# Row-normalised graph product: the adjacency matrix in two slots of 8 MB instead of four of 4 MB, the last wide chunk in half pieces

## The reference

```
N, D, P_DROP = 8192, 64, 0.1
keep = (u >= P_DROP).astype(x.dtype)         # x, u: (8192, 64); adj: (8192, 8192), all float32
x_drop = x * keep / (1.0 - P_DROP)
y = x + jnp.matmul(adj, x_drop)
m = jnp.mean(y, axis=-1, keepdims=True)
v = jnp.var(y, axis=-1, keepdims=True)
return (y - m) / jnp.sqrt(v + 1e-05)
```

## Time and profile before

| | before |
|---|---|
| median of 3 runs | 648.95 us (648.95 to 649.85) |
| profiled execution | 649.06 us |
| its span, first to last instruction | 647.3 us |
| TensorE busy | 503.3 us (78%) |
| VectorE, ScalarE busy | 54.1 us, 17.5 us |
| read from HBM, mean rate | 272.63 MB, 424 GB/s |
| mean granted TensorE clock | 0.953 |

### The profile page before, as it was taken

How to read it: one execution, slowest core, us unless ns; L and a number is a source line. 1 busy time by engine, 2 the same in 40 slices (tenths; PEclk the granted TensorE clock), 3 DMA queues, 4 the chain that set the end, 5 groups by cost and what they waited for, 6 DMA issues and landing times.

```text
span 647.3 us, 5204 instructions
## 1 busy us (share of the span) xinstructions
PE 503.3 (78%) x2308; PEld 177.6 (27%) x2308; DVE 54.1 (8%) x104; ACT 17.5 (3%) x39; POOL 1.3 (0%) x11
## 2 busy tenths in 40 slices
PE   0588878877887977977878877887878868788796
PEld 0132322222222222322222222222322313232463
DVE  1930100001010010100001010010100101000010
ACT  0001000000000000000000000000000000000000
POOL 0000000000000000000000000000000000000000
PEclk9988998899889898899899899889988999889999
DMA  9999999999999999999999999999999999999995
GB/s 369 439 422 437 433 424 435 434 425 432 435 427 433 435 427 431 437 427 431 435 429 436 431 429 429 437 429 429 437 429 429 435 432 427 439 429 425 427 418 233
DMA packets 11817, 274.86 MB, mean 425 GB/s; under 512 B 1312, under 2 KB 1440, under 8 KB 3104
## 3 DMA queue, kind: packets, MB, share of 16 engines
q1 hardware_dynamic: 11088, 272.63, 98.2%
q10 hardware_dynamic: 720, 2.10, 0.8%
HBM read 272.63 MB, written 2.10 MB: 424 GB/s over the span
## 4 chain that ended last, share of the span: by engine, by line
DMA 78%; PE 20%; SPq 1%; issue 0%; another core or an unknown queue 0%; DVE 0%; ACT 0%; DVEq 0%; ACTq 0%
DMA piece<-adj 74%; PE acc L149 20%; DMA piece<-adj_last 4%; SPq L112 0%; SPq L124 0%; PE lifted L208 0%; SPq L109 0%; SPq L108 0%; ACT std L265 0%; DVE rows L335 0%; ACT sums_T L258 0%; DVE stats L329 0%; PE lifted L211 0%; DVE moments L331 0%
## 5 line engine op out<-in xcount | busy, mean ns | idle before, releaser
L149 PE MATMUL acc<-piece,xdrop 128*64 128x512 f32 (+1 forms) x2176 | 486.4, 602 | 139.8 <-DMA piece<-adj 137.4
L149 PEld LDWEIGHTS acc<-piece,xdrop 128*64 128x64 f32 x2176 | 161.6, 143 | 452.7 <-issue 298.7
L303 DVE SCALAR_TENSOR_TENSOR y<-folded,x_sb 128x256 f32<-128x256 f32 (+1 forms) x16 | 6.7, 417 | 555.1 <-PE folded L161 555.1
L229 ACT COPY sums_T<-acc 128x512 f32<-128x512 f32 x15 | 8.8, 585 | 372.0 <-PE acc L149 372.0
L161 PEld LDWEIGHTS folded<-fold,sums_T 128*128 128x128 f32 x124 | 15.0, 191 | 12.1 <-issue 12.1
L161 PE MATMUL folded<-fold,sums_T 128*128 128x64 f32 x124 | 17.2, 281 | 0.0
L221 ACT ACTIVATE std<-square_sum,eps 128x4 f32<-128x4 f32 (+1 forms) x16 | 4.8, 297 | 172.2 <-DVE square_sum L310 172.2
L314 DVE TENSOR_TENSOR rows<-y,rstd 128x256 f32 (+2 forms) x16 | 6.7, 417 | 1.6
L307 DVE TENSOR_TENSOR squares<-y 128x256 f32<-128x256 f32 (+1 forms) x16 | 6.7, 416 | 0.6
L310 DVE TENSOR_REDUCE square_sum<-squares 128x4 f32<-128x256 f32 (+1 forms) x16 | 6.6, 412 | 0.5
L289 DVE SCALAR_TENSOR_TENSOR xdrop<-xdrop,x_sb 128x1024 f32<-128x1024 f32 x4 | 4.9, 1220 | 13.5 <-DMA xdrop<-u 13.5
(11 more groups left out here) (23 smaller groups left out, 5.2 us busy)
## 6 DMA issues: line engine op xcount, KB each, us to landing
piece<-adj SPq DMA_DIRECT2D x60, 4096.0 KB, 31.5
piece<-adj_last SPq DMA_DIRECT2D x1, 3328.0 KB, 28.1
piece<-adj_last SPq DMA_DIRECT2D x1, 2176.0 KB, 31.3
x_sb<-x SPq DMA_DIRECT2D x1, 2048.0 KB, 7.8
xdrop<-u SPq DMA_DIRECT2D x1, 2048.0 KB, 12.2
piece<-adj_last SPq DMA_DIRECT2D x1, 1920.0 KB, 26.5
piece<-adj_last SPq DMA_DIRECT2D x1, 1792.0 KB, 26.4
out<-rows ACTq DMA_DIRECT2D x3, 512.0 KB, 14.8
```

The costliest lines, as they stand in the source:

```text
L149: last = nc.tensor.matmul(acc[i][D * h:D * h + D, 0:cols], xdrop[:, k, :], piece[:, b, :], start=(k < 2), stop=(k >= NB - 2))
L229: nc.scalar.copy(sums_T[:, i, :], acc[i][:, :]).then_inc(sums_copied, 1)
L303: nc.vector.scalar_tensor_tensor(out=y[:, 0:nj, :], in0=folded[i][:, 0:nj, :], scalar=1.0 / KEEP, in1=x_sb[:, bass.ds(block0, nj), :], op0 ...
```

## The change

Each chunk comes in two pieces of 32 blocks instead of four of 16: loads of 8192 KB, 128 rows of 64 KB, in two slots of 64 KB of every partition. The memory taken is the same. A load waits for the piece that lay in its slot one chunk earlier, as before, so one later load can stand in the queue while TensorE works, instead of three. Chunk 14, the last wide one, comes in four half pieces of 4096 KB with a semaphore each (`half_in`); both halves of a slot wait for the whole piece that lay there, and TensorE reports each half done. So the parts of chunk 15 are released after every 16 blocks, as before. The parts keep their sizes and their order; since two slots' parts now lie in one, a row of `adj_last` is 64 KB apart from the next, and was 32 KB. The centring at the start keeps its four quarters. Loads in all: 28 of 8192 KB, 4 of 4096 KB and 15 parts, where there were 60 of 4096 KB and 15 parts.

```
@@ -10,7 +10,7 @@
-SLOTS = 4
+SLOTS = 2
 PB = NB // SLOTS
 NARROW = 2
 LAST_J = J // NARROW
@@ -23,8 +23,12 @@
-PARTS = ((26, 6), (15, 17), (14, 11, 7), (2, 8, 6, 5, 4, 3, 2, 2))
+QUARTERS = 4
+QB = NB // QUARTERS
+HALVES = QUARTERS // SLOTS
+
+
+PARTS = ((26, 6, 15, 17), (14, 11, 7, 2, 8, 6, 5, 4, 3, 2, 2))
...
@@ -113,14 +118,22 @@
             for s in range(SLOTS):
                 load(0, s)
-            with sp.Fori(1, CHUNKS - 1) as c:
+            with sp.Fori(1, CHUNKS - 2) as c:
                 for s in range(SLOTS):
 
                     sp.wait_ge(piece_used, c * SLOTS + (s + 1 - SLOTS))
                     load(c, s)
+
+            for q in range(QUARTERS):
+                s, h = q // HALVES, q % HALVES
+                if h == 0:
+                    sp.wait_ge(piece_used, (CHUNKS - 3) * SLOTS + s + 1)
+                sp.dma_start(pieces[s][:, h * QB:h * QB + QB, :],
+                             adj[(CHUNKS - 2) * SLOTS + s, :, h * QB:h * QB + QB, :]).then_inc(half_in[q], 16)
             for n, (s, b, size) in enumerate(parts):
-                if b == 0:
-                    sp.wait_ge(piece_used, (CHUNKS - 2) * SLOTS + s + 1)
+
+                if b % (LAST_PB // HALVES) == 0:
+                    sp.wait_ge(piece_used, (CHUNKS - 2) * SLOTS + s * HALVES + b // (LAST_PB // HALVES) + 1)
                 sp.dma_start(narrow[s][:, b:b + size, :], adj_last[s, :, b:b + size, :]).then_inc(part_in[n], 16)
...
@@ -169,7 +182,7 @@
             for s in range(SLOTS):
-                pe.wait_ge(dropped, s + 1)
+                pe.wait_ge(dropped, (s + 1) * HALVES)
                 multiply(0, 0, s)
...
@@ -180,7 +193,12 @@
             pe.wait_ge(sums_copied, CHUNKS - 3)
-            wide(CHUNKS - 2, 0)
+            for q in range(QUARTERS):
+                s, h = q // HALVES, q % HALVES
+                pe.wait_ge(half_in[q], 16)
+                products(0, pieces[s][:, h * QB:h * QB + QB, :], q * QB, QB, COLS).then_inc(piece_used, 1)
+                if q == 0:
+                    fold_rows(CHUNKS - 3, 1)
...
@@ -221,8 +239,8 @@
-            def wide(c, i, again=True):
-                act.wait_ge(piece_used, c * SLOTS + SLOTS)
+            def wide(c, i, again=True, used=SLOTS):
+                act.wait_ge(piece_used, c * SLOTS + used)
...
@@ -244,7 +262,7 @@
             for n in range(GROUP - 1):
-                wide(CHUNKS - GROUP + n, n % 2)
+                wide(CHUNKS - GROUP + n, n % 2, used=QUARTERS if n == GROUP - 2 else SLOTS)
```

More of the change, by code:

```diff
@@ L74, in graph_layernorm @@
         piece_in = [sem(f"piece_in{s}") for s in range(SLOTS)]
+        half_in = [sem(f"half_in{q}") for q in range(QUARTERS)]
         part_in = [sem(f"part_in{n}") for n in range(len(parts))]
@@ L201, in _ @@
                             pe.wait_ge(lift_ready, 1)
-                            pe.wait_ge(x_centred, SLOTS)
+                            pe.wait_ge(x_centred, QUARTERS)
                             for j in range(LAST_J):
@@ L272, in quarter @@
             def quarter(q):
-                return slice(q * PB, q * PB + PB)
+                return slice(q * QB, q * QB + QB)
             def centre(out, in_, q, which, ready):
-                n = which * SLOTS + q + 1
+                n = which * QUARTERS + q + 1
                 nc.vector.reduce_sum(node_sum[:, which, quarter(q)], in_[:, quarter(q), :],
@@ L279, in centre @@
                 dve.wait_ge(node_sum_ready, n)
-                sums = node_sum[:, which, quarter(q)].unsqueeze(2).to_broadcast([P, PB, D])
+                sums = node_sum[:, which, quarter(q)].unsqueeze(2).to_broadcast([P, QB, D])
                 nc.vector.scalar_tensor_tensor(out=out[:, quarter(q), :], in0=sums, scalar=-1.0 / D,
@@ L287, in _ @@
             dve.wait_ge(u_in, 16)
-            for q in range(SLOTS):
+            for q in range(QUARTERS):
                 nc.vector.scalar_tensor_tensor(out=xdrop[:, quarter(q), :], in0=xdrop[:, quarter(q), :], scalar=P_DROP,
@@ L293, in _ @@
                 centre(xdrop, xdrop, q, 0, dropped)
-            for q in range(SLOTS):
+            for q in range(QUARTERS):
                 centre(x_sb, x_sb, q, 1, x_centred)
-            dve.wait_ge(x_centred, SLOTS)
+            dve.wait_ge(x_centred, QUARTERS)
             def per_row(v, nj):
```

## The result

The change made the kernel slower: 663.24 us (median of 5 runs, 662.23 to 664.82) against 649.09 us before (5 runs, 648.95 to 649.85), a ratio of 1.0217 with a 95% interval of 1.0206 to 1.0228. The forecast was 647.4 us, the range 646.4 to 653.0. The time lies near what rival C gives for half of its shortfall (667).

What follows compares the result with a forecast made beforehand. The prediction took the kernel to be bound by its loads, one behind the other. From 649.06 us profiled, less 1.5 for fewer loads, plus nothing, came 647.56; the runs' median lying 0.11 lower gave 647.4 us, range 646.4 to 653.

Steps and rivals of the forecast that it cites:

- rival C: Chunk loads: the queue runs dry after twice-slowed pieces, 1.3 us a load, at most 685 us, 667 at half; chance 0.12.
- Less cover: Slots given back after 32 blocks: one later load's 19.42 us transfer hides work and latency, so no load is late; cost nothing.
- The latency: A large load on an empty queue: time beyond its own transfer, bounded between 1.6 and 3.0 us.
- W: TensorE's time on an 8 MB piece, from landing to end: 14.18 us at full clock, 15.87 slowed once, 17.56 twice.
- the formula: Spare time of a reload: 19.28 - W - latency, giving 1.8 to 0.4 us with one slowing, 3.5 to 2.1 at full clock.
- work off the path: TensorE's pieces: nearly every one slowed once by longer waits, 17 us more work, not counted in the time.
- Fewer loads: 28 loads of 8 MB replace 56 of 4 MB: saves 0 to 2.2 us, 1.5 taken; 0.25 if rows are cut.
- The ceiling: DMA rate: 16 ports give 435.2 GB/s, so 8.389 MB takes at least 19.28 us, saving at most 4 us over 28 loads.
- The start: TensorE begins at 32.96 us, a load later; only the first reload waits, issued at 49.0, second piece until 52.4; nothing lost.
- The end: After chunk 13: half pieces land 9.7, 19.4, 29.1 and 38.8 us later, then parts and run-out as before; costs nothing.
- Rival D: Loads with rows 64 KB apart read slower: 5.4 us more (654) at 1%, 38 us more (687) at 7%; chance 0.08.
- Rival B: Loads: nothing to be seen, as rows are cut in two or extra loads cost nothing; 648.7 to 648.95 us; chance 0.30.

Runs made afterwards that it cites:

- the pairs: The kernel before, with its 4 MB loads, but in chunks 0 to 13 two pieces are waited for and given back together: 665.44 us, ratio 1.0258.

## Why the prediction was wrong

The **step that failed** is *Less cover*, in its sentence "So the load is never late, and I cost this at nothing". It was the last term of the sum, and it measured about 16 us instead of 0. Its parts:

- **The latency** of 1.6 to 3.0 us was right: 2.5.
- **The length of a piece** was nearly right. I expected 14.18 us at the full clock and 15.87 with one slowing, on nearly every piece. Measured: 13.95, and 15.3 to 16.9 on 21 of 28. The mean granted clock fell from 0.953 to 0.917. Some pieces were slowed for longer than any before (8.78 - 7.09 = 1.69 us there, up to 16.93 - 13.95 = 2.98 here), most of the way to the second slowing that rival C had named and I had held unlikely.
- **The rule that joined them** was wrong: that a load issued with any spare time at all costs nothing. By W = 15.87 and the measured 2.5 the formula gives 0.9 us to spare, and loads with that much were up to 2.2 us late. What the runs put in its place is a threshold in the cover itself, since the engines that finish early have less of it than the landing shows: above some 5.7 us to the landing of the load ahead nothing is lost, between 4.1 and 5.7 little, under 4.1 most loads are late, by 1 us in the mean. A piece of 15.87 us leaves 19.36 - 15.87 - 0.15 = 3.3 us in these terms, the wrong side of it.

So the loss is of rival C's kind, a queue that runs short, and its chance of 0.12 was too low. But C's condition, W + latency over 19.28, was hardly met: the longest piece and the measured latency give 16.93 + 2.5 = 19.4, and only one other piece comes over 19.28. Nor do "all engines stand still that long": against the kernel with half of the products left out, more of the loss is longer packets (9.7 us) than idle engines (6.9). That the time came out near C's 667 is luck.

**The loop between clock and cover** was seen in the prediction only as work off the path. It is on the path: a longer wait slows the next piece, and its slot comes back later; with the clock mostly kept up 7.6 us came back. The Trainium skill warns of idle gaps between bursts of products (TensorE: Matmul & The Clock Gate, section Why this matters for your kernels); the trace agrees, with waits of up to 7.0 us and the clock of 0.917.

**Fewer loads**: 28 x 0 to 28 x 0.08 = 0 to 2.2 us, of which I took 1.5. Half of the products left out showed 2.2, the upper end. The rows go as whole packets (7056). The ceiling of the Trainium skill (DMA: Bandwidth & Descriptors, section Bandwidth) holds: an undisturbed load of 8.389 MB in 19.36 us runs at 433.3 GB/s, under 435.2.

**The start** was right: TensorE began at 33.01, and the second piece landed at 52.36. **The end** was right only from the fourth half piece on. "Costs nothing" was wrong by 1.9 us: the fourth landed 40.7 us after chunk 13's second piece, not 38.8, by 0.3 us at the first half piece, whose cover was short, and for the rest by the one engine that was late with the third. From the landing of the fourth half piece to the end of the span were 46.2 us before (601.09 to 647.3) and 46.1 after:

```profile
615.39 7.09 PE L162 MATMUL acc<-piece,xdrop 128*64 128x512 f32 x32 [0.94 <-DMA piece<-adj]
```

**Rival D** is excluded by the half loads out of the new layout and by the half products. **Rival B**'s cut rows are excluded by the count of packets, its saving of nothing by the half products.

**Why a load is late with more cover than its latency**, 2.5 to 4.1 us against 2.5, the packets show in part: the cover is measured to the last engine, and the first is done 0.8 to 3.3 us earlier. Excluded are the size of the packets (the pairs lose the same 16.3 us) and a higher latency of the load itself (one at a time). **Open** is why the first rows run longer, up to 3.5 us in the mean instead of 2.4, and what spreads the engines beyond the 0.9 us or so of a fetch. No kernel was run that keeps them in step, so that the spread costs the time, and doesn't only go along with it, is argued from the traces.

## What to carry to other kernels

- A queue of loads needs cover to spare, not just a cover longer than the latency: here 2.5 us of latency wanted some 5.7 us, measured from the issue of a load to the landing of the one ahead. The engines finish a load up to 3.3 us apart, and what counts is the first. Fewer, larger pieces in the same memory save a few hundredths of a microsecond each and shorten this cover by their work; three slots kept both.
- When a change makes TensorE wait longer in one stretch, recompute its work at the lower clock, and put the longer work back into every wait that it releases. It is a loop, and its gain is read by keeping the clock up on purpose.
- Don't take the 9s of the DMA line for a full queue. Multiply the queue's share by the span, and compare both the packet time and the rest.

## What was not expected of the hardware

- The same number of bytes in the same packets took 642.3 us of engine time where loads were issued into a short cover, and 632.6 where not. A packet of 64 KB took 2.42 us in a covered stretch; the first of each engine took 3.5 us in the mean at a short handover and 3.0 on an empty queue.
- The 16 engines finish one load 0.8 to 3.3 us apart, and a single fetch of 16 KB of instructions set one of them back by about 1 us.
- Loads of 4 MB and of 8 MB lose the same 16.3 us when they are given back in steps of 8 MB.
- A load of 8 MB on an empty queue took much the same each time, 21.67 to 22.05 us from issue to landing in the rows shown. On a nearly empty queue its landing varied, with 3.4 to 3.9 us of cover from 0.1 to 2.2 us late; in the first case (landed at 454.68) the first engine was done 2.6 us after the issue, in the second (172.93) 1.3 us.
